# Constant products of TensorE in eight waits of every steady half of a sixteen-graph network kernel

## Time and profile before

| | us |
|---|---|
| median of 3 runs (lowest, highest) | 3496.26 (3494.68, 3502.45) |
| profiled execution, its own time | 3498.6 |
| span in its trace, first to last instruction | 3496.8 |
| TensorE busy | 3099.0 (89%) |
| VectorE busy | 2323.0 (66%) |
| ScalarE busy | 1695.0 (48%) |
| GpSimd busy | 681.2 (19%) |
| DMA traffic | 40.18 MB, 11 GB/s on average |

### The profile page before, as it was taken

The page is one execution under the profiler, slowest core; times in us unless marked ns, Lnnn a source line. Parts: engine busy times, 40 slices in busy tenths (PEclk is TensorE's granted clock), DMA queues, the critical chain, the costliest instruction groups (busy, mean ns, idle before and its releaser), DMA issues.

```text
span 3496.8 us, 54772 instructions
## 1 busy us (share of the span) xinstructions
PE 3099.0 (89%) x20794; PEld 2091.1 (60%) x20794; DVE 2323.0 (66%) x7158; ACT 1695.0 (48%) x3067; POOL 681.2 (19%) x804
## 2 busy tenths in 40 slices
PE   8988988888889888988888888888988888889889
PEld 5755666555565555656555565555656555565577
DVE  3576667767667676667767667676667767667654
ACT  2236454463635536454453645536454463635523
POOL 0012122130221212122131221212122131221202
PEclk9999999999999999999999999999999999999999
DMA  3000000000000000000000000000000000000000
GB/s 129 1 19 1 7 16 4 19 1 7 16 4 19 1 22 1 7 16 4 19 1 7 16 4 19 1 22 1 7 16 4 19 1 7 1 4 4 1 7 5
DMA packets 28742, 40.18 MB, mean 11 GB/s; under 512 B 1344, under 2 KB 17728, under 8 KB 28224
## 3 DMA queue, kind: packets, MB, share of 16 engines
q1 hardware_dynamic: 28480, 36.67, 3.2%
HBM read 28.28 MB, written 4.19 MB: 9 GB/s over the span
## 4 chain that ended last, share of the span: by engine, by line
PE 64%; DVE 18%; ACT 11%; issue 5%; POOL 2%; DVEq 0%
PE ps L438 52%; ACT scratch L1068 7%; DVE scratch L1358 5%; PE ps L904 4%; DVE scratch L1361 3%; DVE scratch L1364 3%; PE ps L447 2%; PE ps L1060 2%; ACT adjf L1068 2%; DVE stats L1379 1%; POOL rstd L2062 1%; ACT L1068 1%; POOL scratch L2085 1%; PE ps L617 1%; ACT xT L1068 1%
## 5 line engine op out<-in xcount | busy, mean ns | idle before, releaser
L1068 ACT ACTIVATE scratch<-scratch 128x512 f32<-128x512 f32 (+4 forms) x768 | 526.1, 688 | 247.8 <-DVE scratch L1358 93.1
L438 PE MATMUL ps<-xT,weights_sb 128*128 128x512 f32 x1152 | 599.6, 636 | 21.3 <-ACT xT L1068 21.2
L438 PE MATMUL ps<-scratch 128*128 128x128 f32 (+6 forms) x4608 | 537.2, 381 | 76.2 <-ACT adjf L1068 35.0
L2085 POOL TENSOR_SCALAR scratch<-scratch 128x512 f32<-128x512 f32 x512 | 351.9, 702 | 1091.9 <-DVE scratch L1862 1091.6
L438 PE MATMUL ps<-weights_sb,scratch 128*128 128x128 f32 (+3 forms) x3840 | 495.6, 280 | 17.9 <-DVE scratch L1364 16.0
L438 PEld LDWEIGHTS ps<-weights_sb,scratch 128*128 128x128 f32 (+3 forms) x3840 | 444.5, 185 | 94.9 <-issue 74.8
L438 PEld LDWEIGHTS ps<-scratch 128*128 128x128 f32 (+5 forms) x4608 | 344.4, 159 | 222.7 <-issue 86.6
L904 PE MATMUL ps<-weights_sb,scratch 128*128 128x128 f32 x2048 | 312.5, 279 | 107.9 <-ACT adjf L1068 68.7
L904 PEld LDWEIGHTS ps<-weights_sb,scratch 128*128 128x128 f32 x2048 | 224.7, 141 | 225.5 <-issue 155.2
L1855 DVE CUSTOM_DVE_ANT_0 scratch<-ps,nomask 128x512 f32<-128x512 f32 x512 | 330.4, 682 | 40.9 <-PE ps L438 40.9
L1068 ACT ACTIVATE scratch<-ps 128x512 f32<-128x512 f32 (+2 forms) x384 | 210.8, 557 | 292.4 <-PE ps L438 204.2
(11 more groups left out here) (166 smaller groups left out, 4534.1 us busy)
## 6 DMA issues: line engine op xcount, KB each, us to landing
adj<-adj SPq DMA_DIRECT2D x16, 1024.0 KB, 5.6
weights_sb<-weights SPq DMA_DIRECT2D x1, 4605.0 KB, 18.9
x_in<-x SPq DMA_DIRECT2D x16, 256.0 KB, 2.8
scratch<-scratch SPq DMA_DIRECT2D x32, 128.0 KB, 2.3
out<-x SPq DMA_DIRECT2D x16, 256.0 KB, 2.3
scratch<-raw SPq DMA_DIRECT2D x1, 1645.0 KB, 22.3
weights_sb<-weights SPq DMA_DIRECT2D x1, 499.0 KB, 6.1
scratch<-raw SPq DMA_DIRECT2D x1, 384.0 KB, 4.8
```

The source lines that it names most:

```text
L438: return pe.matmul(o, lhsT, rhs, start=start, stop=stop, **k)
L1068: return act.activation(o, a, func, **k)
L2085: pool.tensor_scalar(p, p, cut(g, G3_RI + n, 1), 1.0, ALU.mult, ALU.mult).then_inc(s["att_p"], 1)
```

## The change

The string of TensorE's turns in a steady half gets digits between its letters. A digit k calls the new `keep_bank(k)`: two products of the bf16 identity with itself, 128x128, into the first 128 columns of PSUM bank k. With the digits taken out the new string is the old one. There are 76 digits, so 152 products more in each of the 15 steady halves:

| ahead of turn | the wait there | digits | products |
|---|---|---|---|
| 23 | f2's first transpose, on `xn_ready` | 24 x `7` | 48 |
| 27 | f2's projection, on `xT_ready` | 4 x `7` | 8 |
| 71 | f2 across chunks, on `pv_ready` | 3 x `7` | 6 |
| 72 | `g0_back`, on `h_ready` | 24 x `7` | 48 |
| 73 | `f2_out`, on `yg_ready` | 2 x `7` | 4 |
| 84 | `f0_out`, on `half_gap` | 7 x `7` | 14 |
| 185 | `g3_turn`, on `att_p` and `pT_act` | 11 x `3` | 22 |
| 205 | f1's second transpose, on `xn_ready` | 1 x `1` | 2 |

```diff
 PE_TURNS = (
-    "eeeeeeelllllelllllleeeelllllllleeelleeeeeleelllllllllleeeeeeelelelelllllelllleeeeeeeeelelleeeleeeell"
-    "lleeleeeeeleeeeleeeeeleeeeeeeeellleeleeelelllllllleleleeellllllllleeeelllleeleleeleelleleleleeelllll"
-    "lllleeeelellelllleellllelllleeeeellllelleleleellleeleeee"
+    "eeeeeeelllllelllllleeee777777777777777777777777llll7777lllleeelleeeeeleelllllllllleeeeeeelelelellll7"
+    "77l777777777777777777777777e77lllleeeeeee7777777eelelleeeleeeelllleeleeeeeleeeeleeeeeleeeeeeeeelllee"
+    "leeelelllllllleleleeellllllllleeeelllleeleleeleel33333333333leleleleeellllllllle1eeelellelllleelllle"
+    "lllleeeeellllelleleleellleeleeee"
 )
...
-        def halves(turns, early, late, first=None, last=None, prepare=None, keep=None):
+        def halves(turns, early, late, first=None, last=None, prepare=None, keep=None, keep_bank=None):
...
                     if turn == "w":
                         keep(h)
+                    elif turn.isdigit():
+                        keep_bank(int(turn))
                     else:
                         next(run[turn], None)
...
+                def keep_bank(k):
+                    for _ in range(2):
+                        pe.matmul(banks[k][0:P, 0:P], ident_bf[:, :], ident_bf[:, :], start=True, stop=True)
+
-                halves(PE_TURNS, (g0, f0, g1, f1), (g2, f2, g3, f3), PE_FIRST, PE_LAST, prepare, keep)
+                halves(PE_TURNS, (g0, f0, g1, f1), (g2, f2, g3, f3), PE_FIRST, PE_LAST, prepare, keep, keep_bank)
```

## The result

| | before | after |
|---|---|---|
| median, us (lowest, highest, runs) | 3496.71 (3494.68, 3502.45, 4) | 3436.86 (3436.03, 3438.07, 4) |
| span of the profiled execution | 3496.8 | 3436.3 |
| mean granted clock | 0.968 | 0.993 |
| TensorE busy | 3099.0 (89%) | 3160.2 (92%) |
| VectorE, ScalarE busy | 2323.0, 1695.0 | 2320.6, 1692.4 |

The ratio is 0.9826 (95% interval 0.9809 to 0.9844), 60 us less. The forecast was 3436. TensorE is busy for longer than before and the program ends sooner; the other engines do the same work in the same busy time.

A forecast was written before the change was run, and what follows sets the result against it. TensorE bounds the kernel most of the time, partly at half clock. Gains of 35, 19 and 11 us make 65, less 5 for low stretches left: 3496.3 - 60 = 3436 us, range 3426 to 3460.

The forecast's parts named there:

- Place A: Behind f2's transposes, low clock in all 15 halves: segment falls to 14.55 us without it, 35 us gained.
- Place B: Behind `g0_back`, low clock in all 15 halves: segment falls to 5.2 us, VectorE's layernorm next, 19 us gained.
- Place C: Between g3's and g1's pieces late in the half, low clock in seven halves: 11 us, less 5 left.
- The cost of the products: At the eight filled waits: 0 us, each wait keeping some 0.25 us; at most 26 us of latency.
- The clock: In the filled TensorE waits: constant products hold the clock at 1.00, as in half 16; mean granted clock 0.99.
- The pace of 0.08 us a product: Rival at the filled waits: products run slower than 0.056 us, 32 us given back, 3468 us; chance 0.04.
- move to f1's transposes: Rival: the low clock comes once per half around f1's transposes, 25 us instead of 5, 3456 us; chance 0.12.
- The slower rival: At the two long waits: 48 products starting at low clock take 5.1 us, overrunning by 2.2; 3562 us; chance 0.03.

The follow-up runs named there:

- The narrow products: The changed kernel with all 152 constant products a half 16 columns wide instead of 128: 3501.3 us (before 3497.3 in the same session).
- the short fillings alone: The changed kernel without the two runs of 48 products (turns 23 and 72), leaving six fillings, 56 products a half: 3476.3 us.
- The double fillings: The changed kernel with 96 products instead of 48 in each of the two long waits (turns 23 and 72): 3490.4 us.

## Why the prediction was right

**Place A** was put at 14.55 us without low clock and measured 14.57 in all 15 halves. Here the estimate came from halving the busy time of the last low stretch, and it was good because nothing but TensorE was near the path there. The fifteen values of before sum to 254.2 us by the trace, not to the 253.4 of the prediction, and those of the changed kernel to 218.6, so A gave 35.6 us where 35 were forecast.

**Place B** was put at 5.2 us. It shows as 4.81 for the first transpose and 0.43 more behind it (25.25 us from there to g3's first transposes against 24.83), 5.24 in sum. The limit was the one named: `xn` from VectorE comes next, and 0.4 us of TensorE's gain is turned into waiting there. 18.6 us, with 19 forecast.

**Place C**: the sum left three low stretches there, four were found, 6.8 us instead of 5. From g3's first transposes to the next half's f2 the steady halves gave 5.1 us, with 6 forecast (11 less 5). The three kernels with more filling around f1's transposes show that this was the right place and that it can be closed.

**The cost of the products** was taken as nothing. Their pace was 0.0557 us, each wait kept 0.22 to 0.29 us, and the operations that end the waits didn't move. The steady halves, from the first f2 transposes to half 16's, give 59.3 us (A 35.6, B 18.6, C 5.1): 3147.8 us before, 3088.5 after. What lies ahead of them is 1.0 us shorter and what follows 0.2, which makes the 60.5 between the spans. Half 0 isn't edited: it gained by how its low stretches happened to lie. In the traces of the other kernels that part alone differs by up to 6 us. So that the gain is near 60 us is the mechanism's doing; that the time came out within 1 us of the forecast is luck. A steady half is 205.9 us on average, not the 205.7 of the prediction, whose own sum (209.9 less 4.0) gives that too; and its lower bound of 3426 adds up to 3424.

**The clock** was the premise. The narrow products show that without it nothing is gained, and the short fillings alone show a part that the prediction didn't have: at the same place of the fall, the low stretch was 3.4 us long with eight products in the wait behind it and 6.8 without. The prediction needed only the case in which it doesn't fall.

**Rivals.** The pace of 0.08 us a product didn't appear, so the figure of the Trainium skill, "TensorE: Matmul & The Clock Gate", section "Back-to-back issue gap", doesn't hold for these bf16 products on one operand (0.0557 us each, 48 in 2.84 us). The low clock did not move to f1's transposes in every half (four of 15). The slower rival's condition, a low clock when the products start, never came up: all 2280 ran high. The double fillings show how dear it would have been, 53 us for two overruns of 2.3 in every half.

## What to carry to other kernels

Look at the granted clock before anything else where TensorE sets the pace: a mean of 0.968 instead of 0.993 cost 60 us here. The constant products put ahead of a wait on another engine cost nothing here as long as the run of them ended before the wait did, so size it by the wait and the measured pace and leave some 0.2 us. Fill the long waits first and well (two of eight places brought 56 of 60 us), then look where the clock still falls and fill that place.

## What was not expected of the hardware

- Half filled wasn't enough at one long wait and was enough at the other: with 24 products A fell in nine of 15 halves, B in none. The idle rest is about the same (1.6 us). What TensorE does around it differs, and so does the place in time; no run here parts the two.
- The same instructions fall or don't by their place in time. With identical fillings at C, four, five and seven halves fell (the changed kernel, the one with transposes, the one with 36 products), and a short fall shifts all that follows by 1.3 or 1.7 us. One trace in which a place stays high doesn't show that it is safe. With the short fillings alone the halves settled to 208.2 us each, with the same two low stretches in every one.
- One run of 3471.9 us with a mean clock of 0.944 came up among six of a kernel that otherwise took 3428 to 3434. It stays open.
